# Two of GpSimd's three weight differences moved back, and one set of low rows moved from GpSimd to VectorE, in the head of a two-layer convolution kernel

## What is computed

```python
def _L0_conv_ref(x, g_pos, g_neg, bias, input_factor, output_factor):
    v = dac(x * input_factor)              # clip, round to 127 levels
    v = jnp.swapaxes(v, -2, -1)
    v = jnp.pad(v, ((0, 0), (0, 0), (PAD, PAD), (PAD, PAD)))
    patches = unfold2d(v, KH, KW, SH, SW)
    fv = patches + CUBIC * patches ** 3
    g = g_pos - g_neg                      # the weight differences, 3 planes
    outs = [jnp.einsum('bctfyx,ocyx->btfo', fv, g[i]) for i in range(WP - 1)]
    mem_out = adc(outs[-1])
    for i, bit in enumerate(reversed(range(WP - 1))):
        mem_out = mem_out + adc(outs[i]) * 2.0 ** bit
    ...
x = x + _L0_conv_ref(_gn(x), ...)
x = x + _L1_conv_ref(_gn(x), ...)
```

## Time and profile before

| | us |
|---|---|
| median of 3 runs | 1571.08 |
| lowest, highest | 1570.87, 1574.5 |
| the profiled execution | 1572.13 |
| its span, first to last instruction | 1570.1 |
| TensorE busy in it | 1455.7 (93%) |
| VectorE busy | 1394.0 (89%) |
| ScalarE busy | 1158.4 (74%) |
| GpSimd busy | 504.8 (32%) |

### The profile page before, as it was taken

The page is one execution under the profiler, slowest core; times in us unless marked ns, Lnnn a source line. Parts: engine busy times, 40 slices in busy tenths (PEclk is TensorE's granted clock), DMA queues, the critical chain, the costliest instruction groups (busy, mean ns, idle before and its releaser), DMA issues.

```text
span 1570.1 us, 22714 instructions
## 1 busy us (share of the span) xinstructions
PE 1455.7 (93%) x7792; PEld 622.6 (40%) x7792; DVE 1394.0 (89%) x2172; ACT 1158.4 (74%) x1505; POOL 504.8 (32%) x506
## 2 busy tenths in 40 slices
PE   1699999999999999999999999999999999999864
PEld 1354434444443444444344433434443444434322
DVE  6869898999989899998989998898999989898646
ACT  4547778787878788787877887787788868776444
POOL 3111333333333333332332423234242423434212
PEclk9799999999999999999999999999999999999988
DMA  5011012313232131323113141321314132111231
GB/s 202 1 54 40 15 28 54 108 28 107 54 94 53 43 108 28 108 55 107 49 38 103 31 115 46 108 54 35 101 33 115 41 108 54 42 40 41 67 81 54
DMA packets 29173, 103.80 MB, mean 66 GB/s; under 512 B 4032, under 2 KB 4224, under 8 KB 29056
## 3 DMA queue, kind: packets, MB, share of 16 engines
q1 hardware_dynamic: 20416, 70.86, 12.3%
q0 software_dynamic: 8640, 31.46, 10.6%
HBM read 37.29 MB, written 33.55 MB: 45 GB/s over the span
## 4 chain that ended last, share of the span: by engine, by line
PE 74%; DVE 18%; issue 4%; ACT 2%; POOL 1%; DMA 1%; DVEq 0%; SPq 0%; POOLq 0%; ACTq 0%
PE A L483 13%; PE A L485 12%; PE A L484 12%; PE L L543 7%; PE B L483 7%; PE B L484 7%; PE B L485 7%; PE L L587 4%; PE L L574 3%; DVE uall L1127 1%; DVE duo L1045 1%; DVE A L1097 1%; DVE duo L1094 1%; DVE uall L1100 1%; DVE q L1017 1%
## 5 line engine op out<-in xcount | busy, mean ns | idle before, releaser
L483 PE MATMUL A<-T,WH 128*128 128x504 f16 (+1 forms) x1152 | 439.6, 382 | 1.0 <-ACT uall L763 1.0
L484 PE MATMUL A<-T,WH 128*128 128x504 f16 (+1 forms) x1152 | 438.1, 380 | 0.0
L485 PE MATMUL A<-T,WL 128*128 128x504 f16 (+1 forms) x1152 | 438.0, 380 | 0.0
L1364 POOL TENSOR_TENSOR T<-t,T 128x512 f16<-128x512 f32 x192 | 244.5, 1298 | 406.8 <-ACT T L696 406.8
L739 ACT ACTIVATE junk<-xr,shift 128x1024 f16<-128x1024 f32 x248 | 284.7, 1148 | 12.0 <-DVE xr L1130 5.2
L1338 POOL TENSOR_TENSOR zl<-z,zh 128x512 f16<-128x512 f32 x120 | 150.8, 1276 | 397.3 <-ACT zh L796 396.3
L483 PE MATMUL B<-T,WH 128*128 128x504 f16 (+1 forms) x576 | 221.7, 385 | 25.5 <-POOL T L1364 16.3
L485 PE MATMUL B<-T,WL 128*128 128x504 f16 (+1 forms) x576 | 220.6, 383 | 0.9 <-issue 0.9
L484 PE MATMUL B<-T,WH 128*128 128x504 f16 (+1 forms) x576 | 220.9, 384 | 0.0
L483 PEld LDWEIGHTS A<-T,WH 128*128 128x128 f16 x1152 | 115.2, 100 | 195.3 <-issue 82.7
L485 PEld LDWEIGHTS A<-T,WL 128*128 128x128 f16 x1152 | 112.7, 98 | 136.4 <-issue 0.3
(11 more groups left out here) (163 smaller groups left out, 2462.1 us busy)
## 6 DMA issues: line engine op xcount, KB each, us to landing
xr<-in_x_dram SPq DMA_DIRECT2D x64, 512.0 KB, 5.9
out_dram<-xr SPq DMA_DIRECT2D x64, 512.0 KB, 2.7
xr<-shared POOLq DMA_DIRECT2D x60, 512.0 KB, 4.6
xr<-in_L_conv_g_pos_dram SPq DMA_DIRECT2D x3, 576.0 KB, 9.5
xr<-in_L_conv_g_neg_dram SPq DMA_DIRECT2D x3, 576.0 KB, 11.3
xr<-in_L_conv_Wm_dram SPq DMA_DIRECT2D x2, 32.0 KB, 9.7
xr<-in_L_conv_Wq_dram SPq DMA_DIRECT2D x1, 32.0 KB, 11.4
xr<-in_L_conv_Wk_dram SPq DMA_DIRECT2D x1, 32.0 KB, 11.3
```

The costliest lines, as they stand in the source:

```text
L483: nc.tensor.matmul(to, wh, th, start=fresh and y == 1, stop=False, skip_group_check=True)
L484: nc.tensor.matmul(to, wh, tl, start=False, stop=False, skip_group_check=True)
L485: done = nc.tensor.matmul(to, wl, th, start=False, stop=y == 2, skip_group_check=True)
L1364: last = nc.gpsimd.tensor_tensor(low, t32[:, pair, :, :, :].rearrange("p t e w -> p (t e w)"), high, ALU.subtract)
```

## The change

```diff
+            def head_rows_low(g):
+                for pair in range(3):
+                    dve.wait_ge(th_ready, NP * g + pair + 1)
+                    high, low = (T[:, part, pair, g * TILES:(g + 1) * TILES, :, :]
+                                 .rearrange("p t e w -> p (t e w)") for part in range(2))
+                    last = nc.vector.tensor_tensor(low, t32[:, pair, :, :, :].rearrange("p t e w -> p (t e w)"),
+                                                   high, ALU.subtract)
+                last.then_inc(tl_ready, 1)
...
             transform(0, 1, ())
+            head_rows_low(1)
             weight_sums(1)
             phases(dve, phase)
...
             weight_difference(0)
+            scale_x(0)
             weight_difference(1)
-            scale_x(0)
             rows_low(0, 0, 0)
+            pool.wait_ge(sums_made, 2)
             weight_difference(2)
-            rows_low(0, 0, 1)
             phases(pool, phase)
```

## The result

| | median | runs | lowest to highest |
|---|---|---|---|
| before | 1572.41 us | 20 | 1569.8 to 1577.03 |
| changed | 1569.44 us | 20 | 1564.76 to 1573.75 |
| ratio | 0.9977 | | 95% interval 0.9967 to 0.9986 |

The changed kernel is faster, by 3.6 us by this ratio, where I had forecast 6.0, and 1569.44 us lies above the forecast range of 1563.2 to 1567.6. The interval leaves out no change, but 0.23% is under the 0.3% that the prediction asked for before it would say "faster".

The account below looks back on a forecast made before the run. The prediction took the head's relay of waits between engines as the limit, TensorE being busy afterwards. Earlier scale, unblocked transform and VectorE low rows, less a hold-up, gain 6.0 us: 1571.08 - 6.0 = 1565.1 us, range 1563.2 to 1567.6.

Parts of the forecast that it names:

- Step 1: Start of the head: with the scale made earlier, `quantise` and the sums of plane 0 come 2.60 us earlier.
- the two orders: Second difference before L934 and L935, or after them if the scale is held up; less than half a us between.
- Step 2: Second quarter's transform: without the third difference's 2.29 us hold-up it ends at 38.90, 4.9 us earlier.
- Step 3: Second quarter's low rows on VectorE: 0.68 us per subtraction, first product at 41.4, 7.6 us earlier.
- a dear subtraction: Rival at the low rows: VectorE's subtraction costs 1.3 us, as on GpSimd; gain 3.9, 1567.2 us; chance 0.08.
- Step 4: VectorE's queue behind the low rows: third difference holds `cubic_f`; first low weights of plane 1 at 54.0, 6.0 us earlier.
- The rest of the chain: From 59.98 to 70.97 every piece waits for the one before it, so the 6.0 us gain carries through.
- the clock's rival: TensorE's clock falls behind a new 1.6 us pause in the relay, costing 1.7: gain 4.3, 1566.8 us; chance 0.05.
- the sum against the median of the runs shown: Whole kernel: median 1571.08 less the chain's gain of 6.0 gives 1565.1 us, 0.38% less.
- No hold-up: Rival at `cubic_f`: the third difference doesn't hold it up; gain 7.6 us, 1563.5 us; chance 0.12.
- slower: Third difference ends too late for VectorE's sums of plane 2; over 0.3% slower needs an end beyond 75.6; chance 0.03.
- Absorbed later: Rival behind the head: later work that doesn't move with it absorbs the gain, leaving 1571 us; chance 0.06.

Follow-up runs that it names:

- e5: The changed kernel run again unaltered, 12 runs beside the kernel before: 1566.84 against 1572.95 us, ratio 0.9963.
- e1: The kernel before with only the scale moved ahead of the second weight difference: 1570.93 against 1573.60 us, ratio 0.9983.
- e6: The kernel before with only the third difference moved behind the second plane's sums: 1570.94 against 1572.95 us, ratio 0.9985.
- e2: The changed kernel with the second quarter's low rows made by GpSimd again: 1567.13 us against 1573.60 for the kernel before, ratio 0.9967.
- e4: The changed kernel with GpSimd's third difference waiting for the transform of the third quarter: 1566.73 us against 1573.60 for the kernel before, ratio 0.9961.
- e9: The same code as e4, run once more: 1569.76 us against 1574.23 for the kernel before, ratio 0.9970.
- e8: e4 with extra unread matmuls in TensorE's two pauses ahead of its second group of products: 1566.07 us against 1572.95 for the kernel before, ratio 0.9955.

## Why the prediction was wrong in its number and right in most of its steps

- *Step 1.* The scale ended at 18.87 and the second difference ran from 18.84, the second of the two orders that I gave: L934 and L935 went first (in e5's profile it was the other). The sums ended at 22.66, 2.8 us earlier (forecast 2.60, and 22.4 to 22.9 for this order). One detail was other than I wrote: the difference held `quantise` itself (1.48 us for 0.43), not the sums behind it. e1 gives this part 2.5 us of time (+- 0.7).
- *Step 2.* Right to 0.1 us: 38.98 for 38.90. e6 gives it 2.6 us of time (+- 0.7).
- *Step 3.* Right in the price (0.69 for 0.68) and the place (first product at 41.66 for 41.4). The rival of a dear subtraction is out.
- *Step 4.* Right: `cubic_f` held up for 1.2 us, low weights at 54.17 for 54.0. What I did not see is that the third part of the change is then worth nothing (e2): without it, `weight_sums(1)` starts 2.9 us earlier, though GpSimd's low rows stretch it, and VectorE's transform of the third quarter ends at 53.37 instead of 54.26, while ScalarE's cast ends at 54.23 instead of 52.23. The low rows on VectorE bring ScalarE's road forward by 2.0 us and put VectorE's own back by 0.9, and the later of the two ends at 54.2 either way.
- *The rest of the chain.* I carried the 6.0 unchanged from 59.98 to the second group. In the first profile 5.8 became 5.2; in e5, at the full clock, 5.4 stayed 5.4. "Every piece waits for the one before it" was not so: before the change, too, the last low weights of plane 1 start at 70.01 right behind `mix_middle`, when ScalarE's cast had ended at 67.92. That is why of the clock's rival I had the place right, but its price of 1.7 us was too high: a slow second turning hides behind `mix_middle`, and 0.6 us is left.
- *The step that failed is the last one, the sum against the median of the runs shown, with its allowance for few runs.* 1571.08 was the median of three; 71 executions have a mean of 1573.8, 2.7 us more (the median of the 20 beside the change, which hold those three, is 1572.41). The gain was mis-sized by much less: 5.2 us (5.5 at equal clock) for 6.0. The base and the gain alone give 1568.6, already outside the range. I also wrote that "the medians of few runs add one on either side". A single execution in fact scatters with a standard deviation of 2.3 us before and 2.7 after, and the 20 of the changed kernel came out another 0.7 us above the mean of all 32. These parts make up the 4.3 us between 1565.1 and 1569.44: 2.7 of base, 0.8 of gain, 0.8 of scatter.
- *What the sum also took for granted,* that a lead in the head comes out at the end, held in e5's profile (5.7 us) and not in the first one, where the low clock behind 138 us took 1.6 and the last 85 us took 3.1. On the average of the executions it held to within 1 us.
- *No hold-up* and *slower* are out: the hold-up stands in the rows, and the third difference ended at 49.37, 16 us before VectorE's sums of plane 2 wanted it (65.67). *Absorbed later* is out too, as a rule; in single executions the clock does just that.

What stays open: why one pause lowers the clock and the same pause in another execution doesn't, why sets of the same code differ by about 1 us at equal clock, and whether e4's 1.1 us is in the time.

## What to carry to other kernels

A gain at the head of a relay is worth what reaches the last wait of it, so each part has to be followed to the place where another engine's release comes last; when a part shortens one of two roads of equal length and lengthens the other, it is worth nothing, however well it does its job at the place where it is put. A GpSimd instruction that was in VectorE's way should go where VectorE reads PSUM or waits (in e4 and e9 the third difference then held up nothing in the rows), and not merely behind the next wait, where it held `cubic_f`. And before forecasting a change of 0.3%, look at how the runs of one kernel spread and with what: here the us at the low clock go with most of the spread inside a kernel, and a base of three runs was off by half of the effect.

## What the runs showed of the hardware

A `tensor_scalar` with a single SBUF input, int16 to f16 on 1,024 elements, took 1.48 us beside GpSimd's difference in the changed kernel (1.49 in e1, 1.80 in e2, each time ending 0.3 us behind GpSimd's end) and 0.43 without, so it is held up as instructions with two inputs are. The Trainium skill says that `tensor_scalar` can, when its operands allow it, enter a mode in which it takes the port pair that VectorE shares with GpSimd ("SBUF — State Buffer", section "Who interferes with whom"); the row agrees. On the other hand `low_weights`, with one input in PSUM, took 0.96 us in e9 where it started just ahead of the third difference (53.38 and 53.41), the same as alone, and the difference behind it took 2.62 us, as the 2.61 of the earlier trace rows.

The granted clock fell in different places in executions of the same code. In the turnings at 56 us, behind a pause of 1.84 us, it was 0.55 in one profile of the changed kernel, and the turnings ran at full speed behind 2.54 us in the other. Behind the pause of 2.2 us that ends at 138 us it fell in one and not in the other. Behind the pause of 2.0 us ahead of the third group it was 0.62 in e8 and 1.00 in e9, which have the same code from the second group on.
